# A mixture-of-experts stage: a unit's index tables made in eight pieces instead of in one chain

## What is computed

```python
for _ in range(2):
    z_norm = rmsnorm(z, norm_w)
    scores = softmax(z_norm @ router_w)                 # 8 experts
    topk_vals, topk_idx = top_k(scores, 2)              # two experts per token
    cw = sum(one_hot(topk_idx, 8) * topk_vals / (sum(topk_vals) + 1e-9))
    for e in range(8):
        mixed += cw[:, e] * ((silu(z_norm @ w1[e]) * (z_norm @ w3[e])) @ w2[e])
    z = z + mixed
```

## Time and profile before

| what | value |
|---|---|
| median of 3 runs | 2308.6 us (2305.61 to 2311.1) |
| profiled execution | 2307.91 us, span 2306.2 us |
| mean granted TensorE clock | 0.959 |
| PE / DVE / ACT / POOL busy over the span | 2011.8 / 1844.3 / 1462.1 / 1232.1 us |
| expert stage, first tile's transpose to the last | 1600.0 to 2252.4 us |
| indirect DMAs of GpSimd, scatters and gathers | 256 at 977 ns and 256 at 980 ns |

### The profile page before, as it was taken

The page is one execution under the profiler, slowest core; times in us unless marked ns, Lnnn a source line. Parts: engine busy times, 40 slices in busy tenths (PEclk is TensorE's granted clock), DMA queues, the critical chain, the costliest instruction groups (busy, mean ns, idle before and its releaser), DMA issues. The chain is left out here.

```text
span 2306.2 us, 47356 instructions
## 1 busy us (share of the span) xinstructions
PE 2011.8 (87%) x14679; PEld 982.9 (43%) x14679; DVE 1844.3 (80%) x5277; ACT 1462.1 (63%) x3354; POOL 1232.1 (53%) x1710
## 2 busy tenths in 40 slices
PE   5999999999988999899999999974888988988991
PEld 1222222222222465444444444432555766766661
DVE  8999999999999576888888888847777676676555
ACT  1788888888888332677777777751545655655550
POOL 6343343343321021676767676634476777667776
PEclk9999999999999999899999999985999999999996
DMA  7355344344341001434232433302233443433453
GB/s 183 102 130 139 102 130 139 102 129 139 102 129 48 1 19 37 100 70 101 69 99 71 96 74 93 76 26 74 87 106 101 122 117 114 118 108 113 130 139 99
DMA packets 224610, 226.94 MB, mean 98 GB/s; under 512 B 34032, under 2 KB 187504, under 8 KB 224368
## 3 DMA queue, kind: packets, MB, share of 16 engines
q1 hardware_dynamic: 152432, 164.62, 27.0%
q0 software_dynamic: 16384, 33.59, 5.0%
q10 hardware_dynamic: 55552, 25.71, 3.9%
HBM read 96.48 MB, written 125.76 MB: 96 GB/s over the span
## 5 line engine op out<-in xcount | busy, mean ns | idle before, releaser
L702 ACT ACTIVATE mid_PT<-mid_ps 128x512 f32<-128x512 f32 (+2 forms) x1792 | 914.0, 568 | 258.4 <-PE mid_ps L583 250.5
L785 DVE TENSOR_REDUCE mid_nmax<-mid_ps 128x1 f32<-128x512 f32 (+2 forms) x1280 | 776.4, 657 | 61.5 <-PE mid_ps L562 36.4
L562 PE MATMUL mid_ps<-KT,QT 48*128 48x512 bf16 (+3 forms) x2048 | 604.5, 351 | 68.3 <-DVE mid_nmax L785 49.6
L583 PE MATMUL mid_ps<-QT,KT 64*128 64x512 bf16 (+3 forms) x2048 | 562.5, 346 | 2.5 <-ACT mid_PT L702 2.2
L599 PE MATMUL mid_ps<-mid_PT,vv 128*32 128x512 f32 (+3 forms) x4096 | 465.1, 527 | 16.3 <-POOL mid_PT L914 12.5
L562 PEld LDWEIGHTS mid_ps<-KT,QT 48*128 48x128 bf16 x2048 | 158.9, 94 | 585.2 <-DVE mid_nmax L785 397.4
L782 DVE CUSTOM_DVE_ANT_0 mid_PT<-mid_ps,mask 128x512 bf16<-128x512 f32 (+1 forms) x512 | 304.5, 619 | 68.8 <-PE mid_ps L562 64.0
L1395 PE MATMUL moe_ps<-moe_w,moe_xinT 128*128 x638 | 341.5, 618 | 0.0
L1506 POOL DMA_INDIRECT rows_in<-moe_xn,moe_scat_idx x256 | 250.2, 977 | 161.9 <-DVE moe_scat_idx L1696 86.0
L1519 POOL DMA_INDIRECT moe_yg<-rows_out,moe_gat_idx x256 | 250.8, 980 | 80.6 <-issue 77.2
L1450 ACT ACTIVATE moe_xinT<-moe_ps,norm_w 128x128 f32<-128x128 f32 x319 | 116.7, 366 | 275.8 <-PE moe_ps L1407 186.9
(11 more groups left out here) (266 smaller groups left out, 3060.0 us busy)
## 6 DMA issues: line engine op xcount, KB each, us to landing
l_spread<-mid_slots SPq DMA_DIRECT2D x128, 384.0 KB, 5.4
rows_in<-mid_blank SPq DMA_DIRECT2D x64, 512.0 KB, 3.8
QT<-l_spread SPq DMA_DIRECT2D x128, 192.0 KB, 4.3
KT<-l_spread SPq DMA_DIRECT2D x128, 192.0 KB, 5.2
moe_xin<-rows_in SPq DMA_DIRECT2D x319, 64.0 KB
rows_out<-moe_y ACTq DMA_DIRECT2D x319, 64.0 KB
x<-in_L_attn_x_dram SPq DMA_DIRECT2D x8, 512.0 KB, 6.6
QT<-mid_mrows SPq DMA_DIRECT2D x256, 6.0 KB
```

Source lines behind the costliest of these rows:

```text
L562: mm = pe.matmul(ps[:, bank, n_keys * a:n_keys * (a + 1)], QT[rows, par, pair, i * P:(i + 1) * P], KT[rows, par, pair, 0:n_keys], start=Tr ...
L583: mm = pe.matmul(ps[:, bank, m * a:m * (a + 1)], KT[rows, own, pair, i * P:(i + 1) * P], QT[rows, own, pair, SEQ - m:SEQ], start=True, sto ...
L702: act.activation(weights_of(r, i, heads), ps[:, ring(S2, n - 2, k), 0:widths[i] * len(heads)], ACT.Exp, scale=scale).then_inc(exp_done, 1)
L785: dve.tensor_reduce(to, of, X_AXIS, ALU.max, negate=True).then_inc(s1_used, 1)
```

## The change

STAGES stays 20, and TABLES = 8 further stages are added to each group. They come at `begin + s * length // 20` with s = 20 to 27: in loop 1 one on each tile of the eight from begin + 20 on, in loop 0 at begin + 14, 14, 15, 16, 16, 17, 18, 18. For the last group of a unit they do a piece of the tables each; for all others they are empty. The instructions are the same in the same order, except that the running sum is cleared in piece 0 and not after the words. SP no longer waits for `tables` at a unit's first tile but for the new signal `rows_made`, which piece 5 gives when rows and words are there. GpSimd waits for `tables` as before. The piece of unit u before or beside the stages of the next group stands first where both fall on one tile.

```diff
-    STAGES = 20
+    STAGES, TABLES = 20, 8
...
-        return [(k, s) for k, at in begin.items() for s in range(STAGES) if at + s * length(k) // STAGES == n]
+        return [(k, s) for k, at in begin.items() for s in range(STAGES + TABLES) if at + s * length(k) // STAGES == n]
...
-                    sp.wait_ge(tables, u + 1)
+                    sp.wait_ge(rows_made, u + 1)
...
-                    if k + 1 == first_of[unit_of[k]] + sizes[unit_of[k]]:
-                        make_tables(unit_of[k])
-
-            def make_tables(u):
+                if s >= STAGES and k + 1 == first_of[unit_of[k]] + sizes[unit_of[k]]:
+                    make_tables(unit_of[k], s - STAGES)
+
+            def make_tables(u, part):
...
+                if part == 0:
+                    c.link(dve.tensor_scalar(full_u, iota_f[:, 0:ht].unsqueeze(1).to_broadcast([P, EXPERTS, ht]),
+                                             float(P), None, ALU.mult))
+                    c.link(dve.tensor_tensor(full_u, count.unsqueeze(2).to_broadcast([P, EXPERTS, ht]), full_u, ALU.is_gt))
+                    dve.memset(run_sum[:, :], 0.0)
+                    c.link(dve.tensor_reduce(ntiles[:, :], full_u, X_AXIS, ALU.add))
+                if part == 1:
+                    c.link(dve.tensor_tensor(pair[:, :, :], tri[:, :, :], per(ntiles[:, :], EXPERTS), ALU.mult))
...
+                if part == 2:
+                    c.link(dve.tensor_tensor(passed_u, iota_f[0:1, 0:n_tiles].unsqueeze(2).to_broadcast([1, n_tiles, EXPERTS]),
+                                             per(last_t[0:1, :], n_tiles, 1), ALU.is_ge))
...
+                if part == 3:
+                    dve.tensor_reduce(before, shares_u, X_AXIS, ALU.add)
+                    c.link(dve.tensor_reduce(expert, passed_u, X_AXIS, ALU.add))
+                if part == 4:
+                    c.link(dve.tensor_tensor(before, iota_f[0:1, 0:n_tiles], before, ALU.subtract))
...
+                if part == 5:
+                    own = slice(base_of[u], base_of[u] + n_tiles)
+                    dve.tensor_tensor(row_of[0:1, own], row, live, ALU.mult)
...
+                    dve.tensor_copy(words[0:1, word_of[u]:word_of[u + 1]], sums[:, 0:n_words]).then_inc(rows_made, 1)
+                    dve.wait_ge(rows_made, u + 1)
+                if 6 <= part < 6 + n_it:
+                    k = first_of[u] + part - 6
...
+                    if part == 5 + n_it:
+                        last.then_inc(tables, 1)
+                        dve.wait_ge(tables, u + 1)
+                    else:
                         c.link(last)
```

More of the change, by code:

```diff
@@ L1297, in experts @@
         ones = sb("ones", [P, P], BF16)
-        const, w_in = sem("const"), sem("w_in")
+        const, w_in, rows_made = sem("const"), sem("w_in"), sem("rows_made")
         x_loaded = [sem(f"x_loaded{s}") for s in range(RING)]
@@ L1325, in run @@
             for k in range(EARLY):
-                for s in range(STAGES):
+                for s in range(STAGES + TABLES):
                     side(k, s)
@@ L1697, in side @@
                     dve.wait_ge(scat_ready, k + 1)
-                    if k + 1 == first_of[unit_of[k]] + sizes[unit_of[k]]:
-                        make_tables(unit_of[k])
-            def make_tables(u):
+                if s >= STAGES and k + 1 == first_of[unit_of[k]] + sizes[unit_of[k]]:
+                    make_tables(unit_of[k], s - STAGES)
+            def make_tables(u, part):
                 count, n_it, n_tiles = run_sum[:, :], sizes[u], tiles_in[u]
-                ht = IT * n_it
+                ht, n_words = IT * n_it, words_in[u]
@@ L1705, in make_tables @@
                 full_u, passed_u, shares_u = full[:, :, 0:ht], passed[:, 0:n_tiles, :], shares[:, 0:n_tiles, :]
+                expert, before, live, row = (tab[:, a, 0:n_tiles] for a in range(4))
                 def per(t, n, k=P):
                     return t.unsqueeze(1).to_broadcast([k, n, EXPERTS])
-                c.link(dve.tensor_scalar(full_u, iota_f[:, 0:ht].unsqueeze(1).to_broadcast([P, EXPERTS, ht]),
-                                         float(P), None, ALU.mult))
-                c.link(dve.tensor_tensor(full_u, count.unsqueeze(2).to_broadcast([P, EXPERTS, ht]), full_u, ALU.is_gt))
@@ new lines, in make_tables @@
+                if part == 1:
+                    c.link(dve.tensor_tensor(pair[:, :, :], tri[:, :, :], per(ntiles[:, :], EXPERTS), ALU.mult))
+                    c.link(dve.tensor_reduce(base[:, :], pair[:, :, :], X_AXIS, ALU.add))
+                    dve.scalar_tensor_tensor(move[:, :], base[:, :], float(P), region[:, :], ALU.mult, ALU.subtract)
+                    c.link(dve.tensor_tensor(last_t[:, :], base[:, :], ntiles[:, :], ALU.add))
+                if part == 2:
+                    c.link(dve.tensor_tensor(passed_u, iota_f[0:1, 0:n_tiles].unsqueeze(2).to_broadcast([1, n_tiles, EXPERTS]),
+                                             per(last_t[0:1, :], n_tiles, 1), ALU.is_ge))
+                    c.link(dve.tensor_tensor(shares_u, passed_u, per(ntiles[0:1, :], n_tiles, 1), ALU.mult))
@@ new lines, in make_tables @@
+                if part == 3:
[3 more added lines that the diff above has]
+                    c.link(dve.tensor_tensor(before, iota_f[0:1, 0:n_tiles], before, ALU.subtract))
+                    dve.tensor_scalar(before, before, float(P), None, ALU.mult)
+                    dve.tensor_scalar(live, expert, EXPERTS - 0.5, None, ALU.is_lt)
+                    c.link(dve.tensor_scalar(row, expert, float(CAP), None, ALU.mult))
+                    c.link(dve.tensor_tensor(row, row, before, ALU.add))
@@ new lines, in make_tables @@
+                if part == 5:
+                    own = slice(base_of[u], base_of[u] + n_tiles)
+                    dve.tensor_tensor(row_of[0:1, own], row, live, ALU.mult)
+                    code = coded[:, :, :].rearrange("o c i -> o (c i)")[:, 0:n_tiles]
+                    c.link(dve.tensor_tensor(code, expert, live, ALU.mult))
+                    c.link(dve.tensor_tensor(weighted[:, 0:n_words, :], coded[:, 0:n_words, :], places[:, 0:n_words, :], ALU.mult))
+                    c.link(dve.tensor_reduce(sums[:, 0:n_words], weighted[:, 0:n_words, :], X_AXIS, ALU.add))
+                    dve.tensor_copy(words[0:1, word_of[u]:word_of[u + 1]], sums[:, 0:n_words]).then_inc(rows_made, 1)
+                    dve.wait_ge(rows_made, u + 1)
@@ L1744, in make_tables @@
                                              moved_by[:, :].rearrange("p (a t) -> p a t", a=2), ALU.add)
-                    if k + 1 < first_of[u] + n_it:
+                    if part == 5 + n_it:
+                        last.then_inc(tables, 1)
+                        dve.wait_ge(tables, u + 1)
+                    else:
                         c.link(last)
-                last.then_inc(tables, 1)
-                dve.wait_ge(tables, u + 1)
             run(tile, side, 0)
```

## The result

| | before | changed |
|---|---|---|
| median | 2309.61 us (4 runs) | 2290.32 us (4 runs, 2290.0 to 2292.12) |
| span of the profiled execution | 2306.2 | 2288.3 |
| mean granted TensorE clock | 0.959 | 0.965 |
| VectorE busy | 1844.3 | 1843.4 |

The ratio is 0.9921, 95% interval 0.9904 to 0.9938. The prediction was 2287, range 2273 to 2300.

What follows compares the result with a forecast made beforehand. The expert stage was taken as bound by TensorE except at the tables, with gains passing through GpSimd's waits: 17.7 us up to tile 220 plus 3.0 at g21 and g22 gave 20.7, from 2307.91 to 2287.2; range 2273 to 2300.

Steps and rivals of the forecast that it cites:

- Same work: Whole kernel: all instructions stay, one signal is added and the clearing moves up; 0 +- 0.5 us in all.
- Loop 1: Units 4 to 8: spread tables leave shorter waits; gains of 3.3, 3.2, 3.3, 4.3 and 4.3 us.
- summed lateness at unit 4: Tiles 115 to 122: VectorE's pieces and group 9's work add 6.4 us of lateness, leaving 4.5 us of waiting.
- the price of the old stand: TensorE's half clock after each unit's tables before the change, taken as 2.3 us per unit on top of the wait.
- Loop 0: Units 1 to 3, where pieces share tiles with group stages: gains of 0.8, 5.8 and 1.3 us.
- Unit 1: TensorE at tile 23: the load after scatter s2 limits the gain to at most 0.8 us, taken as 0.8.
- s2 ends as before: Scatter s2 before unit 1's loads: its index is made at tile 13 as before, so its end does not move.
- Through GpSimd: GpSimd's queue: s5, s12 and s13 come 6.6, 14.4 and 17.7 us earlier; waits before g21 and g22 give 3.0 more.
- The clock rule as a rival: TensorE at tiles with pieces and adds: half clock stays on in spread waits, 2333 us; chance 0.06 slower, 0.02 no change.
- Later rows_made: SP's load of each unit's first tile: it waits for the scatter anyway, so the later signal costs 0.

Runs made afterwards that it cites:

- third try: Each unit's tables in one chain and groups 10 to 14 started 1 to 7 tiles earlier, against the kernel before: 2308.1 us beside 2308.0, ratio 1.0000.

## Why the prediction was right, and where it was off

*Same work.* Right: VectorE's busy time 1844.3 and 1843.4, and one chain with the new signal is within 0.1% of before.

*Loop 1.* Right, a little low. Gains by the transposes of the tiles around each unit: 3.05, 4.40, 3.39, 5.26 and 4.96 us for units 4 to 8, forecast 3.3, 3.2, 3.3, 4.3 and 4.3. The summed lateness at unit 4 was 1863.28 - 1846.98 - 6 x 1.63 = 6.5 us (forecast 6.4). The loss that stayed was sized well too: by the steps 4.8, 4.2, 4.1 and 3.4 us at units 4 to 7, forecast 4.5, 4.5, 4.5 and 3.5. Only 3.2 of unit 4's 4.8 show as waits, because a late step is longer by some 0.26 us than its wait. What was low is the price of the old stand: I took 2.3 us of clock for every unit, while by the steps the old units 5, 7 and 8 had lost 3 and more.

*Loop 0.* Unit 2 gained 5.3 (forecast 5.8) and unit 3 0.5 (1.3, with 0 as the lower end). The wait for z was 3.55 us in unit 1, up from 1.20, and 1.93 in unit 3, up from 0.32.

*Unit 1* is the term that failed: +0.8 forecast, -1.7 measured (-0.5 to -1.7 over seven profiles). Two steps were wrong. "s2 ends as before": the last DMA of s2 was issued 0.9 us later along the stage, behind the DMA of 1.95 us. The load itself took 1.7 us to land (I had 2), so without that delay TensorE could have gained the 0.8; with it, tile 23 gained 0.1. And I priced the early arrival at nothing: the step behind the stand took 3.40 us for 1.63, of which the half clock is the larger part, since after a stand of 1.05 us at full clock it took 2.26.

*Through GpSimd.* Right in its mechanism, and 3 us too high at each scatter: s5 came 3.4 us earlier (forecast 6.6), s12 11.4 (14.4), s13 14.8 (17.7), and 2.7 more came at g21 to g23, forecast 3.0. The waits left before s12 and s13 were 4.27 and 3.69 us, forecast 4.1 and 3.5. Counted from tile 13 it was 15.0 at s13; of the missing 2.7 unit 1 has 2.5, units 2 and 3 1.3 and unit 4 0.2, less 1.3 that units 5 and 6 gave more. Units 7 and 8 gained 10.2 us that the end did not get but for the last two waits, as said. The kernels with groups earlier, with and without spread tables, show that it is GpSimd's queue that ends last with spread tables, and TensorE without.

*The clock rule as a rival.* By the rule of the Trainium skill ("TensorE: Matmul & The Clock Gate", section "A second HAM failure mode: psum-queue depth-cycling") frequent short idles might have held the clock down. At the slices of 0.2 to 0.9 us of units 4 to 7, and at unit 8's 1.42 and 1.87, the rows show full clock throughout, so there the rule did not bear on it. In loop 0, where waits of 2 to 3.6 us came in a row, half clock did come back, for a step or two after the 2.72 of the load, the 3.01, and the 2.36, 0.45 and 1.93 of unit 3. I had priced that for units 1 and 3 only in part and for unit 2 not at all. *Later rows_made* cost 0, as forecast.

## What to carry to other kernels

A long chain on an engine that feeds a pipeline costs what exceeds the pipeline's tolerance, plus the clock after the stand. Spreading it pays by where the work falls, not by how small the pieces are: add up per tile what the engine has to do, and put the pieces beside the empty stages. Price what stays by the length of the steps, not by the waits in them. Before pricing a gain, follow it through the second-longest chain, with every wait in it, because that gives the part that reaches the end and names the next edit (here, starting groups earlier, which gave 7 us and was worth nothing before the change). And price an early arrival too: an engine that comes early to a fixed transfer stands, and TensorE then paid 0.5 to 1.7 us for the stand.

## What I had not expected of the hardware

Whether a wait of 2 to 3.6 us costs clock differs from execution to execution at the same place of the program. The wait for z in unit 1 took 3.55 us in the changed kernel, and the product behind it ran at full clock; it took 3.56 in the kernel in which SP waits for all tables, and the product behind it took 1.92 us:

```profile
1641.24 0.66 PE L1424 MATMUL moe_ps<-ident,z 128*128 128x128 f32 x4 [3.56 <-DVE z L1635]
...
1642.38 1.92 PE L1395 MATMUL moe_ps<-moe_w,moe_xinT 128*128 x2
```

Waits of 2.01 and of 2.23 us fell on either side too. In the twelve profiles every wait of 3.7 us and more in the expert stage was followed by half clock within two steps. Even a short wait can be: in the repeat of the changed kernel three steps at full clock stand before this wait of 1.41 us, and half clock behind it.

```profile
1658.77 0.33 PE L1407 MATMUL moe_ps<-ident,moe_xin 128*128 128x128 f32 x1 [1.41 <-DMA moe_xin<-rows_in]
...
1659.63 1.75 PE L1395 MATMUL moe_ps<-moe_w,moe_xinT 128*128 x2
```

At unit 1 it made a difference of some 1.1 us from execution to execution. And in two rounds the kernel before took 2755 and 2757 us in place of 2308. The first of them and the third try, with 2308, both name chip 6, so it is not shown that this belongs to a chip, as I had taken it. The profiles there are of the kernel with one chain and groups earlier: the attention part has its usual speed (tile 0 at 1602.5 and 1601.8), and the expert stage takes 1.7 times as long. The longest stop of TensorE is 19 us in the one and 23 in the other. The profile puts it down to ScalarE, which stands as long itself, for nothing that the profile names; VectorE and SP stand in the same stretch, GpSimd goes on. What does that is open.
